# The last norm moved into the grouped-attention loop of a 16-image hybrid kernel

## The reference, cut to what matters

```python
t = t + _L3_attn_ref(_ln_t(t), Wq, bq, Wk, bk, Wv, bv, Wo, bo)
t = t + _L3_ffn_ref(_ln_t(t), gate_w, experts)
# _ln_t(v): (v - mean) / sqrt(var + 1e-5) over the 128 channels of a token
# _L3_attn_ref: scores of 8 groups x 4 heads, softmax over the 8 groups, weights summed
# over all tokens of an image, then one 128x128 matrix A per image times the normed tokens
```

## Time and profile before

| | us |
|---|---|
| median of 3 runs | 4942.04 |
| their range | 4937.94 to 4942.81 |
| the profiled execution's own time | 4943.43 |
| its span in the trace | 4941.8 |
| from the last residual of the grouped attention to the first instruction of the routing | 83.42 |

### The profile page before, as it was taken

One profiled execution on the slowest core, in us unless ns is written; L12 is line 12 of the kernel. 1 busy time (PEld: TensorE's weight loads), 2 busy tenths in 40 slices (PEclk: granted clock), 3 DMA queues, 4 the chain that ended last, 5 costly groups with the idle time before them and its releaser, 6 DMA issues. The chain is left out here.

```text
span 4941.8 us, 75311 instructions
## 1 busy us (share of the span) xinstructions
PE 4227.2 (86%) x23034; PEld 1655.7 (34%) x23035; DVE 2891.6 (59%) x5461; ACT 2186.0 (44%) x4040; POOL 1827.6 (37%) x1333
## 2 busy tenths in 40 slices
PE   5799999756999999999999999977999999876513
PEld 2343434233222222222222222224444444453312
DVE  4788888666877767676767677523000000256774
ACT  3333333155366656565656566654444444431400
POOL 1100000046277767676767677872000000120401
PEclk9999999978799999999999999988999999966655
DMA  3555556258122222222222222011000000111504
GB/s 137 139 131 124 137 120 137 74 206 236 23 32 32 32 33 33 33 32 33 32 33 32 33 32 32 8 43 46 0 0 0 0 0 0 68 65 40 198 0 149
DMA packets 185054, 313.43 MB, mean 63 GB/s; under 512 B 44279, under 2 KB 103677, under 8 KB 182285
## 3 DMA queue, kind: packets, MB, share of 16 engines
q1 hardware_dynamic: 155400, 270.21, 23.5%
q10 hardware_dynamic: 24960, 28.87, 1.7%
q0 software_dynamic: 4368, 10.07, 0.7%
HBM read 102.88 MB, written 78.12 MB: 37 GB/s over the span
## 5 line engine op out<-in xcount | busy, mean ns | idle before, releaser
L1678 DVE TENSOR_REDUCE at_mx<-at_side 128x1 f32<-128x512 f32 x2048 | 1294.9, 683 | 415.1 <-PE at_side L1581 404.2
L1752 ACT ACTIVATE at_P<-at_S 128x512 f32<-128x512 f32 x2048 | 1120.3, 600 | 750.3 <-PE at_S L1613 700.1
L1511 POOL TENSOR_TENSOR at_pairs<-at_P 128x2048 f32<-128x2048 f32 x256 | 1160.2, 4532 | 317.0 <-ACT at_P L1752 296.5
L1613 PE MATMUL at_S<-at_qo,at_ko 99*128 99x512 bf16 x2048 | 786.1, 388 | 75.1 <-ACT at_P L1752 75.1
L1581 PE MATMUL at_side<-at_ko,at_qo 96*128 96x512 bf16 x2048 | 789.2, 398 | 44.0 <-DMA at_ko<-qk 23.2
L2034 ACT ACTIVATE ff_hs<-ff_ph,ff_b 128x512 f32<-128x512 f32 x512 | 351.7, 687 | 524.2 <-PE ff_ph L2004 524.2
L1624 PE MATMUL at_num<-at_P,at_rvt 128*32 128x512 f32 x4096 | 551.6, 611 | 0.0
L2004 PE MATMUL ff_ph<-ffn_Y,ff_w 128*128 (+1 forms) x1024 | 524.8, 595 | 8.7 <-DMA ff_b<-in_b_dram 8.7
L2018 PE MATMUL ff_po<-ff_hs,ff_w2s 128*128 128x512 f32 x1024 | 522.9, 593 | 0.0
L2053 DVE SCALAR_TENSOR_TENSOR X<-ff_po,ffn_b2w,X 128x512 f32 (+1 forms) x32 | 24.0, 751 | 822.7 <-PE ff_po L2018 822.7
L834 DVE SCALAR_TENSOR_TENSOR la_dwq<-la_pad,la_taps,la_dwq 128x1024 f32<-128x1024 f32 x384 | 491.5, 1280 | 11.1
(11 more groups left out here) (416 smaller groups left out, 4542.6 us busy)
## 6 DMA issues: line engine op xcount, KB each, us to landing
la_rep<-la_pad SPq DMA_DIRECT2D x512, 162.8 KB, 3.6
qk<-ap_part SPq DMA_DIRECT2D x32, 768.0 KB, 3.7
at_qo<-qk SPq DMA_DIRECT2D x192, 128.0 KB, 4.7
at_ko<-qk SPq DMA_DIRECT2D x192, 128.0 KB, 7.6
n_ln_xs<-X SPq DMA_DIRECT2D x96, 256.0 KB, 2.3
u<-ap_us SPq DMA_DIRECT2D x32, 320.0 KB, 4.0
X<-in_x_dram SPq DMA_DIRECT2D x4, 2048.0 KB, 22.7
conv<-conv_Y SPq DMA_DIRECT2D x16, 512.0 KB, 2.6
```

Of the source, the lines that this page charges most:

```text
L1511: g.tensor_tensor(pairs[i % 2][:, :, :], P[a][:, :, :], P[a + 1][:, :, :], ALU.add).then_inc(pair_done, 1)
L1613: pe.matmul(S[n % RING][:, :], ko[u][:, h, j * C:(j + 1) * C], qo[u][:, h, half * CH:(half + 1) * CH], start=True, stop=True).then_inc(s_r ...
L1678: v.reduce_max(mx[:, n // 2, n % 2:n % 2 + 1], side[bank][:, :], AX.X).then_inc(side_saved, 1)
L1752: a.activation(P[k % SLOTS][:, i, :], S[(4 * k + i) % RING][:, :], ACT.Exp).then_inc(p_ready, 1)
```

## The change

`phase_gqa` becomes `phase_gqa_norm`. Its loop runs over steps s; step s still holds the attention of image s (with the same looks ahead), and between its parts stand the parts of n4's chunks 2s-6 to 2s-1, that is of the images two and three steps back. Two chunks are in flight instead of four. The result goes in place into Y, whose old columns are no longer needed; that copy is on ACT instead of DVE, the DMA of the tokens is on SP's queue instead of ACT's. `front` shares its banks with `pv`, and `back` has two banks (`ln.back` and `pc`). The separate phase n4 and its barrier go; Y is allocated once for both. `vector_stats` is also changed for its three other users: its wait on `ab_ready` stands ahead of the statistics instead of between them and their aggregation. The diff, cut to its core:

```diff
     def vector_stats(self, v, n, u):
         v.wait_ge(self.front_ready, n + 1)
+        wait_if(v, self.ab_ready, n - self.r + 1)
         for r in range(4):
             last = v.bn_stats(self.st[u][:, r, :], self.front[u][:, r, :])
...
-        wait_if(v, self.ab_ready, n - self.r + 1)
         for r in range(4):
             last = v.bn_aggr(self.mv[u][:, r, :], self.st[u][:, r, :])
...
+        def pipeline(eng, step, drain):
+            for s in range(4):
+                step(s, s % 2, False)
+            with eng.Fori(2, B // 2 - 2) as i:
+                for u in range(2):
+                    step(2 * i + u, u, False)
+            for s in range(B - 4, B + drain):
+                step(s, s % 2, s >= B - 1)
...
             def _(sp):
...
+                def step(s, u, last):
+                    if before(s + 3, B):
+                        images(s + 3, 1 - u)
+                    if among(2 * s - 2):
+                        chunk_in(2 * s - 2, 0)
+                    if among(2 * s - 5):
+                        chunk_out(2 * s - 5, 1)
+                    if among(2 * s - 1):
+                        chunk_in(2 * s - 1, 1)
+                    if among(2 * s - 4):
+                        chunk_out(2 * s - 4, 0)
...
             def _(pe):
...
+                def channels(n, u):
+                    pe.wait_ge(ln.xt_ready, n + 1)
+                    wait_if(pe, ln.saved, n - 1)
+                    for r in range(4):
+                        last = pe.transpose(back[u][:, r * C:(r + 1) * C], ln.xt[u][:, r, :], K["ident"][:, :])
+                    last.then_inc(ln.back_ready, 1)
+                def step(s, u, last):
+                    if before(s + 2, B):
+                        scores(s + 2, u)
+                    if among(2 * s - 6):
+                        channels(2 * s - 6, 0)
+                    if among(2 * s - 4):
+                        ln.tensor_front(pe, 2 * s - 4, 0)
+                    if before(s, B):
+                        outputs(s, u)
+                    if among(2 * s - 5):
+                        channels(2 * s - 5, 1)
+                    if among(2 * s - 3):
+                        ln.tensor_front(pe, 2 * s - 3, 1)
+                    if before(s + 1, B) and not last:
+                        sums(s + 1)
...
             def _(a):
...
+                def normal(n, u, save_n):
+                    if among(save_n):
+                        a.wait_ge(ln.back_ready, save_n + 1)
+                    if among(n):
+                        wait_if(a, tok_out[u], 8 * (n - u))
+                        ln.scalar(a, n, u)
+                    if among(save_n):
+                        a.copy(Y[:, bass.ds(save_n * CH, CH)], back[u][:, :]).then_inc(ln.saved, 1)
+                def step(s, u, last):
+                    if before(s + 1, B) and not last:
+                        powers(s + 1)
+                    normal(2 * s - 5, 1, 2 * s - 7)
+                    normal(2 * s - 4, 0, 2 * s - 6)
...
             def _(v):
...
-                    if not last:
-                        below_max(b + 1, st)
-                    if not isinstance(b, int) or b:
-                        residual(b - 1, 1 - u)
-                    mixing(b, u, st)
-                    if not last:
-                        weights(b + 1, st)
+                def step(s, u, last):
+                    if not isinstance(s, int) or s:
+                        residual(s - 1, 1 - u)
+                    st = Chain(v, dstep, NW * s + FIRST)
+                    if before(s + 1, B):
+                        below_max(s + 1, st)
+                    if among(2 * s - 4):
+                        ln.vector_stats(v, 2 * s - 4, 0)
+                    if before(s, B):
+                        mixing(s, u, st)
+                    if before(s + 1, B):
+                        weights(s + 1, st)
+                    if among(2 * s - 3):
+                        ln.vector_stats(v, 2 * s - 3, 1)
+                pipeline(v, step, 1)
...
-            phase_norm(nc, K, X, Y, "n4", D["tokens"])
```

More of the change, by code:

```diff
@@ L2080, in gqa_load, with phase_gqa_norm @@
         eng.dma_start(W[name][:, :], D[name]).then_inc(w_in, 16)
-def phase_gqa(nc, K, D, X, Y, W, w_in, sums):
+def phase_gqa_norm(nc, K, D, X, Y, W, w_in, sums, tokens):
     GH = G8 * H4
@@ L2104, in phase_gqa @@
         top = m.sb("top", [C, TL * H4])
-        pa = m.ps("pa", [C, CH])
+        ln = LayerNorm(m, K, X, 2)
+        pa, pv = ln.back, ln.front
         pc = m.ps("pc", [C, CH])
-        pv = [m.ps(f"pv{h}", [C, 4, C]) for h in range(2)]
+        back = [ln.back, pc]
+        tok_out = [m.sem("tok_out0"), m.sem("tok_out1")]
         psc = m.ps("psc", [C, TL, GH])
@@ L2120, in y_count, with among, before @@
             return (b // 2 + 1) * 16 if isinstance(b, int) else 8 * b + (16 - 8 * u)
+        def among(n):
+            return not isinstance(n, int) or 0 <= n < NCH
+        def pipeline(eng, step, drain):
[6 more added lines that the diff above has]
+                step(s, s % 2, s >= B - 1)
+        def before(b, end):
+            return not isinstance(b, int) or b < end
         with nc.Block() as block:
@@ L2124, in _, with images, chunk_in, chunk_out @@
             def _(sp):
-                def step(b, u, last):
+                def images(b, u):
                     wait_if(sp, s_mm, b - 1)
                     sp.dma_start(ys[u][:, :], Y[:, bass.ds(b * N, N)]).then_inc(y_in[u], 16)
-                over(sp, B, step)
+                def chunk_in(n, u):
+                    if isinstance(n, int) and n < 2:
+                        sp.wait_ge(x_ready, n + 1)
+                    else:
+                        sp.wait_ge(ln.mv_ready, n - 1)
+                    sp.dma_start(ln.xs[u][:, :], X[:, bass.ds(n * CH, CH)]).then_inc(ln.staged[u], 16)
+                def chunk_out(n, u):
+                    sp.wait_ge(ln.xt_ready, n + 1)
+                    sp.dma_start(tokens[bass.ds(n * CH, CH), :].rearrange("(r p) c -> p r c", p=C), ln.xt[u][:, :, :])\
+                      .then_inc(tok_out[u], 16)
+                def step(s, u, last):
[9 more added lines that the diff above has]
+                        chunk_out(2 * s - 4, 0)
+                for b in range(3):
+                    images(b, b % 2)
+                pipeline(sp, step, 3)
+                for u in range(2):
+                    sp.wait_ge(tok_out[u], 16 * NCH // 2)
+            @block.gpsimd
+            def _(g):
+                over(g, NCH, lambda n, u, last: ln.gpsimd(g, n, u))
             @block.tensor
@@ L2172, in _, with outputs @@
                 scores(1, 1)
-                def step(b, u, last):
-                    if not isinstance(b, int) or b + 2 < B:
-                        scores(b + 2, u)
+                def outputs(b, u):
                     pe.wait_ge(a_ready, b + 1)
@@ L2180, in step, with powers @@
                         pe.matmul(po[h][:, :], A[u][:, 0:C], Y[:, bass.ds(b * N + h * CH, CH)], start=True, stop=True).then_inc(o_mm, 1)
-                    if not last:
-                        sums(b + 1)
-                over(pe, B, step)
+                def channels(n, u):
[19 more added lines that the diff above has]
+                        sums(s + 1)
+                pipeline(pe, step, 3)
             @block.scalar
             def _(a):
-                with a.Fori(0, B) as b:
+                def powers(b):
                     a.wait_ge(sub_ready, b + 1)
                     a.activation(sc[:, :, :], sc[:, :, :], ACT.Exp, scale=C ** -0.5).then_inc(e_ready, 1)
+                def normal(n, u, save_n):
[11 more added lines that the diff above has]
+                    normal(2 * s - 4, 0, 2 * s - 6)
+                powers(0)
+                pipeline(a, step, 4)
             @block.vector
@@ L2265, in _ @@
                 FIRST = st.n
-                def step(b, u, last):
-                    st = Chain(v, dstep, NW * b + FIRST)
-                    if not last:
-                        below_max(b + 1, st)
-                    if not isinstance(b, int) or b:
-                        residual(b - 1, 1 - u)
-                    mixing(b, u, st)
-                    if not last:
-                        weights(b + 1, st)
-                        assert st.n == NW
-                over(v, B, step)
-                residual(B - 1, 1)
+                def step(s, u, last):
[10 more added lines that the diff above has]
+                        weights(s + 1, st)
+                        assert st.n == NW
+                    if among(2 * s - 3):
+                        ln.vector_stats(v, 2 * s - 3, 1)
+                pipeline(v, step, 1)
+                for n in range(NCH - 2, NCH):
+                    ln.vector_stats(v, n, n % 2)
 E8 = 8
@@ L2720, in build @@
             phase_ffn(nc, K, D, X, Y, wcol, b2w)
-        with Mem(nc, "gqa") as m:
+        with Mem(nc, "late") as m:
             Y = m.sb("Y", [C, T])
[L2723 to L2728, removed]
```

(6 more changed lines are left out.)

## The result

| | median us | runs | ratio to before, 95% interval |
|---|---|---|---|
| before | 4942.43 | 4937.94 to 4946.82 | |
| after | 5008.06 | 5005.29 to 5013.68 | 1.0134 [1.0117, 1.0152] |

The change makes the kernel 1.3% slower, 66 us; forecast were 5014 us, 72 slower. The profiled execution has a span of 5004.9 us, 63.1 more than before.

A forecast was written before the change was run, and what follows sets the result against it. A chain of DVE and PE waiting for each other bounds the loop, 10.28 us per image. 13 longer steps cost 134 us, the drain some 20, only 83 are saved: 72 us slower, 5014 us, range 4975 to 5032.

The forecast's parts named there:

- The order: Merged loop: DVE's and PE's written orders put scores, transposes and statistics on the chain, about 20.6 us per image against 10.28.
- Every sign that the prediction named: New timeline: DVE idle about 6 us after the subtraction, some 4 behind `weights`; `outputs` about 3.6; subtractions 20 to 21 apart.
- The clock: PE in the merged loop: scores, first transposes and outputs at half clock, after pauses of about 2.7 and 5.2 us.
- the second transposes: Back and front transposes behind the outputs: taken as 1.57 us, the middle of half clock 2.01 and full clock 1.12.
- Rival (a): Merged loop: PE at full clock throughout, step 15.27 us, 4940 us in all, no change; chance 0.07.
- Rival (b): Merged loop: the scores alone at full clock, step 18.44 us, 4986 us in all; chance 0.20.
- step before image 3's subtraction: Loop start: a residual of 1.40 us leaves this step, so the third subtraction moves from 4425.17 to 4423.8.
- step 2: First merged step counted: no back transposes, so 20.6 - 0.91 - 0.69 = 19.0 us.
- steps 3 to 13: Middle of the merged loop: each step counted at 20.6 us.
- step 14, step 15 and drain: Loop end: one more step at 20.6 us, then 30.6 us without scores, with the norm's whole latency three times in a row.
- steps 3 to 14: 12 x 20.6: Merged loop: twelve equal steps of 20.6 us, 247.2 us in all.
- The drain: Loop end together with step 15: 31.0 us, or 30.6 from the step's border, including 13.4 for two passes of the norm's latency.

## Why the prediction was right

**The order.** Right at each place. Every sign that the prediction named is in the timeline: DVE idle 6.61 us behind the subtraction, ended by L1076, and 3.83 behind the weights, outputs of 3.57 (4514.07 to 4517.64), steps of 20.45. Moving the statistics, moving the sums and halving the scores show that the order causes it. All three raised the clock too (0.71, 0.74, 0.67), but with the clock at 1.00 this order still takes 15.29 us a step, 5 more than the kernel before.

**The clock.** Right in what came, not in all of its ground. Scores, first transposes and outputs run at 0.50, and the second transposes begin where the clock rises: from their start to the statistics 4519.03 - 4517.64 = 1.39, taken as 1.57, the middle of 2.01 and 1.12, a choice between two values that happened to lie close. Rival (a), full clock for an image in 15.27 us, is what the kernel with matmuls in both of PE's pauses measures: 15.29. Rival (b), the scores alone at full clock, did not come: they take 4.48 us. But the prediction chose the clock of scores and outputs by the length of the pauses alone. The pause ahead of the scores, which it put at about 2.7 us, is 3.4 to 4.0, in part because the sums take 0.60 us there and not 1.06. And length alone does not decide: with the statistics behind the mixing, scores began at full clock after a pause of 3.43. That they ran at half here was in part luck.

**The sum, against the measured terms:**

| term | forecast | measured | from |
|---|---|---|---|
| step before image 3's subtraction | -1.4 | -1.06 | 8.92 against 9.98 |
| step 2 | 19.0 | 18.22 | 4421.52 to 4439.74 |
| steps 3 to 13 | 226.6 (11 x 20.6) | 224.94 | 4439.74 to 4664.68 |
| step 14, step 15 and drain | 51.2 (20.6 + 30.6) | 46.38 | 4664.68 to 4711.06, end of the last copy |

**The mis-sized term** is "steps 3 to 14: 12 x 20.6". Step 14 is not like the others: the scores run two images ahead, so it issues none, which the prediction saw only for step 15. From the end of the residual ahead of it (4664.32) to the next one's (4678.03) it took 13.7 us, 6.9 less than counted. The drain gave 2.0 of that back: from 4678.03 to 4711.06 it is 33.0, where 31.0 was forecast. These 4.8 us with the other terms (0.8 and 1.7 less, 0.3 more) are the difference between the 72 us and the some 65 that the trace shows: 62.35 between the last copies (4711.06 - 4648.71), and 2.59 by which this kernel is ahead at image 2's subtraction already. The latter is no gain of the change: image 0's subtraction varies by 6 us from run to run (4394.81 here, 4400.78 with the statistics behind the mixing). The drain's 2.0 lie in part in ACT's copy to Y (L2270, 0.6 us): PE's back transposes there wait for it, which the term left out, and the two passes of the norm's latency took 7.6 and 7.9 us instead of 6.7 each. The rows of the two residuals and of one such wait:

```profile
4662.94 1.38 DVE L2349 SCALAR_TENSOR_TENSOR X<-gq_po,gq_A,X 128x512 f32<-128x512 f32 x2
...
4676.65 1.38 DVE L2349 SCALAR_TENSOR_TENSOR X<-gq_po,gq_A,X 128x512 f32<-128x512 f32 x2
...
4701.51 1.09 PE L2235 MATMUL gq_pc<-ident,gq_ln_xt 128*128 128x128 f32 x4 [2.97 <-ACT late_Y L2270]
```

**The table load.** The prediction allowed ACT one table load of 1.28 us a step, hidden. There is one in the whole loop, and as the others would have been hidden, it made no difference:

```profile
L2260 ACT ACT_TABLE_LOAD x1 | 1.3, 1283 | 3.5 <-PEq L57 3.5
```

## What to carry to other kernels

Idle time on two engines that wait for each other in turn is room for more work only where that work stays off the chain: an instruction put into the gap waits in its engine's order for its own input, and everything behind it on the chain waits too. Before moving work into a loop, write down each engine's order and ask of each inserted instruction whether its input was made a step earlier; the same inserted work cost 66 us in one order and won 60 in another. Where a longer chain leaves PE standing still, look at the granted clock as well: here a full clock alone took a step from 20.45 to 15.29 us.

## What the runs showed that was not expected

- Matmuls whose result is thrown away shortened the step by a quarter, from 20.45 to 15.29 us, as the granted clock went from 0.59 to 1.00.
- The pause right before an instruction does not tell its clock by itself. With the statistics behind the mixing, the scores' first matmul ran at full clock (0.69 us) after a pause of 3.43; in the kernel after it took 1.22 after a pause of 3.44 (4522.77, the last row of the step's timeline). What else decides was not tried.
- Exponentials in a step with copies and scalings loaded ACT's table once in the whole loop; the loop of before, where the exponential was ACT's only work, loaded it 16 times, 20.5 us in all. Why was not tried.
